# Two products with V side by side on TensorE, and one ScalarE copy for both

## The chip, the cores and the metric

The kernel runs on one core of one Trainium2 chip. The metric is the device time of one execution in microseconds (us), and the median of several executions is compared.

## The reference

The input is x of shape (16, 256, 256): 16 sequences of 256 tokens with 256 features. Three stages follow each other, each on a layer norm of x and added back to x.

```python
x = x + 0.5 * ffn(layernorm(x))     # 16 experts, each token goes to its best 2
x = x + attention(layernorm(x))     # 16 heads of 16, causal
x = x + 0.5 * ffn(layernorm(x))
```

The change touches attention only. For each batch (sequence) and head it computes `softmax(q k^T / 4 + causal mask) v`, the outputs of 16 heads are joined to 256 features and multiplied by `w_out`.

## The kernel before

Five engines run programs of their own and meet at semaphores: TensorE (PE) multiplies, VectorE (DVE) and ScalarE (ACT) read its outputs out of the eight banks of its output memory, GpSimd (POOL) masks and gathers rows, SyncE (SP) issues transfers. In attention the 16 batches are pipelined by hand. Each engine has a written-out order of steps (`PE_TURN`, `ACT_TURN`, `DVE_TURN`, `POOL_TURN`, `SP_TURN`), and `batches` runs through that list once per turn. An entry is (offset, kind, number): in turn i the step is done for batch i + offset, if there is such a batch. So one turn of PE holds steps of several batches. The waits are in the steps themselves (`after(engine, semaphore, count)`), and an engine that waits holds everything behind it in its list.

The steps of one batch that matter here:

- SCORE 0 to 11 (line 440, and one mask product at line 443). PE makes query by key scores in two banks in turn (bank 3 and 4), 4 heads at a time for n under 4 and 2 heads for the others. DVE takes the row maximum of each (line 590, also called SCORE). SCORE n on PE waits for the reduce of SCORE n-2 (`max_ready`), since it uses its bank.
- T 0 to 11 (line 465). PE makes the scores again, transposed (key by query), in banks 0, 1 and 2 in turn. ACT takes the exponential of each into `pr0` or `pr1` (line 537, also called T); both have two buffers. T n on PE waits for the exponential n-3. The exponentials of T 3g on ACT wait for the product PV g-2, which has read the same buffer.
- MASK on POOL (line 370) clears half a tile after the exponentials 1, 2, 4, 5, 7, 8, 10 and 11. Between these stand FETCH steps (line 346), which gather rows for a later batch.
- PV 0 to 3 (line 479). For a group of four heads PE multiplies the exponentials with V, each head in a strip of 32 columns of the array, into one half of `bankC`. PV n waits for 2n+2 masks. ACT copies that half to `oT` (line 525, also called PV), and the next PV waits for the copy.
- UN 0 and 1 (line 487) transpose `oT` back once all four copies are done (`oT_ready`). Then follow the division by the row sum on DVE (lines 608 and 610), TR and PR (lines 494 and 499), the product with `w_out`.
- V (line 427) makes V of a batch two later than the one whose PV stand in the same turn. ACT copies it (line 521) to `v_sb[b % 2]`, the buffer which the PV of that earlier batch read:

```python
elif kind == V:
    after(act, at["v_done"], b + 1)
    after(act, at["pv_done"], G * (b - 1))
```

- Q and K (line 420) multiply by the query and key weights, NORM (line 408) transposes the layer norm's output; ACT copies it (line 508). DVE splits q and k into bf16 parts: `LEFT_K` is line 580, `LOW_Q` and `LOW_K` line 585. In `DVE_TURN`, LEFT_K stands between the reduces of SCORE 3 and 4, LOW_Q between 5 and 6, and MIX (four instructions, lines 553 and 558, for a later batch) between 7 and 8.

Of the kernel before, what the change touches and what calls it, by code (L numbers as in the profile page):

```python
# [16 lines left out]
def macaron_block(nc, x_in, w_qkv, w_out, gate_w, gate_up, down, out, stages=("ffn", "attn", "ffn")):  # L17
    B, S, H = x_in.shape
# [30 lines left out]
    G = HEADS // 4  # L49
# [10 lines left out]
    with ctx:  # L60
# [124 lines left out]
        oT = sb("oT", [P, HEADS // 4, S])  # L185
# [89 lines left out]
        def exists(j):  # L275
# [9 lines left out]
        FETCH, MIX, MOMENTS, ROOT, NORM, Q, K, V = "fetch", "mix", "moments", "root", "norm", "q", "k", "v"  # L285
        HI_Q, HI_K, LEFT_Q, LEFT_K = "hi q", "hi k", "left q", "left k"
        MID_Q, MID_K, LOW_Q, LOW_K = "mid q", "mid k", "low q", "low k"
        SCORE, MAX, T, MASK, PV, UN, TR, PR = "score", "max", "scoreT", "mask", "pv", "untranspose", "transpose", "project"
        STATS = "stats"

        PE_TURN = [(-1, SCORE, 3), (-2, T, 5), (-2, T, 6), (-1, SCORE, 4), (-2, PV, 0), (-1, SCORE, 5), (-2, T, 7),
                   (-2, T, 8), (-1, SCORE, 6), (-2, T, 9), (-1, SCORE, 7), (-2, PV, 1), (-2, T, 10), (-2, T, 11),
                   (-1, SCORE, 8), (-1, SCORE, 9), (-2, PV, 2), (0, V, 0), (-2, PV, 3), (-1, SCORE, 10), (1, NORM, 0),
                   (-1, SCORE, 11), (-2, UN, 0), (-2, UN, 1), (1, Q, 0), (-1, MAX, 0), (-2, TR, 0), (1, K, 0),
                   (-2, TR, 1), (-2, PR, 0), (-2, PR, 1), (0, SCORE, 0), (-1, T, 0), (0, SCORE, 1), (-1, T, 1),
                   (-1, T, 2), (-1, T, 3), (0, SCORE, 2), (-1, T, 4)]
        ACT_TURN = [(12, MID_Q, 0), (12, HI_K, 0), (10, T, 0), (10, T, 1), (10, T, 2), (10, T, 3), (10, T, 4),
                    (10, T, 5), (10, T, 6), (10, PV, 0), (10, T, 7), (10, T, 8), (10, PV, 1), (10, T, 9), (10, T, 10),
                    (10, T, 11), (10, PV, 2), (12, MID_K, 0), (10, PV, 3), (12, V, 0), (13, NORM, 0), (11, MAX, 0),
                    (13, HI_Q, 0), (10, TR, 0), (10, TR, 1)]  # L300
        DVE_TURN = [(17, SCORE, 7), (20, MIX, 0), (17, SCORE, 8), (17, SCORE, 9), (18, LOW_K, 0), (20, MOMENTS, 0),
                    (17, SCORE, 10), (17, SCORE, 11), (16, UN, 0), (17, MAX, 0), (16, UN, 1), (20, NORM, 0),
# [17 lines left out]
        def after(eng, s, n):  # L320

            if n > 0:
                eng.wait_ge(s, n)
# [72 lines left out]
        def attn_tensor(pe):  # L396
# [5 lines left out]
            def part(kind, n, b):  # L402
# [8 lines left out]
                elif kind in (Q, K):  # L411
                    x, dst = OF[kind], (bankB, bankA)[OF[kind]]
                    after(pe, at["anT_ready"], b + 1)
                    if kind == Q:
                        after(pe, at["v_ready"], b)
                        if b == 0:
                            pe.wait_ge(ffn[0]["ye_ready"], NE_T)
                    for e in range(2):
                        for c in range(HC):
                            last = nc.tensor.matmul(dst[:, e * S:(e + 1) * S], wqk[:, c, x, e, :], anT[:, c, :],  # L420
                                                    start=(c == 0), stop=(c == HC - 1))
                    last.then_inc(at["qk_done"], 1)
                elif kind == V:
                    after(pe, at["left_ready"], 2 * b + 1)
                    for u in range(2):
                        for c in range(HC):
                            last = nc.tensor.matmul(bankB[:, u * H:(u + 1) * H], anT[:, c, u * P:(u + 1) * P], wv[:, c, :],  # L427
                                                    start=(c == 0), stop=(c == HC - 1))
                    last.then_inc(at["v_done"], 1)
                elif kind == SCORE:  # L430
                    u, h0, nh = score_of(n)
                    if n == 0:
                        after(pe, at["stacked_q"], 16 * SLOTS * (b + 1))
                        after(pe, at["stacked_k"], 16 * SLOTS * (b + 1))
                        after(pe, at["nmaxT_ready"], b)
                    after(pe, at["max_ready"], 3 * G * b + n - 1)
                    dst, w = bank[3 + n % 2], P * (u + 1)
                    q, k = qT[b % BUFS], kT[b % BUFS]
                    for i in range(nh):
                        nc.tensor.matmul(dst[:, i * w:(i + 1) * w], q[0:ROWS, h0 + i, u * P:(u + 1) * P], k[0:ROWS, h0 + i, 0:w],  # L440
                                         start=(i == 0), stop=False, skip_group_check=True)
                    diag = dst[:, :].rearrange("p (h k) -> p h k", k=w)[:, :, u * P:(u + 1) * P]
                    nc.tensor.matmul(diag, ident_b[:, :], future[:, 0:nh, :], start=False, stop=True,  # L443
                                     skip_group_check=True).then_inc(at["score_done"], 1)
                elif kind == MAX:
                    after(pe, at["nmax_ready"], b + 1)
                    for u in range(2):
                        last = nc.tensor.transpose(bank[3][:, :].bitcast(BF16)[0:3 * HEADS, u * P:(u + 1) * P], nmax[:, u, :],
                                                   ident_b[:, :])
                    last.then_inc(at["nmax_transposed"], 1)  # L450
                elif kind == T:
                    kt, h0, nh = scoreT_of(n)
                    if n == 0:
                        after(pe, at["maxed"], 16 * (b + 1))
                    if n < 2:
                        after(pe, at["x_done"], 2 * b + n - 1)
                    elif n == 2:
                        after(pe, at["attT_ready"], 2 * b)
                    else:
                        after(pe, at["exp_ready"], 3 * G * b + n - 2)  # L460
                    dst, w = bank[n % 3], S - kt * P
                    q, k = qT[b % BUFS], kT[b % BUFS]
                    for i in range(nh):
                        h = h0 + i
                        last = nc.tensor.matmul(dst[:, i * w:(i + 1) * w], k[0:ROWS + 3, h, kt * P:(kt + 1) * P],  # L465
                                                q[0:ROWS + 3, h, kt * P:S], start=(i == 0), stop=(i == nh - 1),
                                                skip_group_check=True)
                    last.then_inc(at["scoreT_done"], 1)
                elif kind == PV:
                    after(pe, at["masked"], 2 * G * b + 2 * n + 2)  # L470
                    after(pe, at["oT_ready"], G * b + n)
                    if n == 0:
                        after(pe, at["v_ready"], b + 1)
                        after(pe, at["attT_ready"], 2 * b - 1)
                    cols = n % 2 * S
                    for kt in range(2):
                        for j in range(4):
                            rhs = pr0[n % 2][:, j, :] if kt == 0 else pr1[n % 2][:, j, :]
                            last = nc.tensor.matmul(bankC[j * VW:(j + 1) * VW, cols + kt * P:cols + S],  # L479
                                                    v_sb[b % 2][:, kt, 4 * n + j, :], rhs, start=(kt == 0), stop=(kt == 1),  # L480
                                                    skip_group_check=True)
                    last.then_inc(at["pv_done"], 1)
                elif kind == UN:
                    after(pe, at["oT_ready"], G * (b + 1))
                    after(pe, at["exp_ready"], 3 * G * b + 10 + n)
                    for g in range(G):
                        last = nc.tensor.transpose(bank[n][:, g * P:(g + 1) * P], oT[:, g, n * P:(n + 1) * P], ident[:, :])  # L487
                    last.then_inc(at["o_transposed"], 1)
                elif kind == TR:
                    after(pe, at["att_ready"], 2 * b + n + 1)  # L490
                    if n:
                        after(pe, at["exp_ready"], 3 * G * (b + 1))
                    for c in range(HC):
                        last = nc.tensor.transpose((bankC, bank[2])[n][:, c * P:(c + 1) * P], att[:, n, c * P:(c + 1) * P], ident[:, :])
                    last.then_inc(at["att_transposed"], 1)
                elif kind == PR:
                    after(pe, at["attT_ready"], 2 * b + n + 1)
                    for c in range(HC):
                        last = nc.tensor.matmul(bank[n][:, 0:H], attT[:, n, c, :], wout_sb[:, c, :], start=(c == 0), stop=(c == HC - 1))  # L499
                    last.then_inc(at["proj_done"], 1)  # L500
            batches(PE_TURN, part)

        def attn_scalar(act):
            def part(kind, n, b):
# [17 lines left out]
                        .then_inc(at["v_ready"], 1)  # L522
                elif kind == PV:
                    after(act, at["pv_done"], G * b + n + 1)
                    nc.scalar.copy(oT[:, n, :], bankC[:, n % 2 * S:(n % 2 + 1) * S]).then_inc(at["oT_ready"], 1)
                elif kind == MAX:
                    after(act, at["nmax_transposed"], b + 1)
                    after(act, at["maxed"], 16 * b)
# [1 line left out]
                elif kind == T:  # L530
                    kt, h0, nh = scoreT_of(n)
                    g = n // 3
# [864 lines left out]
```

## Time and profile before

| | |
|---|---|
| median of 3 executions | 798.5 us (795.11, 798.5, 799.29) |
| the profiled execution | 797.04 us, span 795.3 us |
| PE busy over the span | 646.0 us (81%) |
| DVE, ACT, POOL busy | 517.8, 404.8, 398.1 us |
| granted clock of TensorE, mean | 0.914 |

The span reaches from the first to the last instruction; the execution's own time is 1.74 us longer. Busy times of engines overlap. The products PV stand in the trace from 246.3 to 546.5 us, and between them lie the 16 turns of attention that hold one batch's PV each.

### The profile page before, as it was taken

How to read it: one execution, taken by the hardware profiler on the slowest of the kernel's cores; microseconds unless marked ns; L12 is line 12 of the kernel's file. 1: busy time of each engine (PE TensorE's matmuls, PEld its weight loads, DVE VectorE, ACT ScalarE, POOL GpSimd, SP SyncE). 2: the span in 40 equal slices, each digit the busy share in tenths (PEclk: the TensorE clock that was granted, in tenths of full speed). 3: DMA queues.
4: the chain of work that ended last, by engine and by line, in shares of the span. 5: the costliest groups of instructions: out<-in, count | busy, mean ns of one | idle time of the engine just before them, and what ended most of it. 6: DMA issues, size and time to landing. Idle time of an engine off the chain costs nothing.

```text
span 795.3 us, 18007 instructions
## 1 busy us (share of the span) xinstructions
PE 646.0 (81%) x5502; PEld 526.3 (66%) x5503; DVE 517.8 (65%) x1407; ACT 404.8 (51%) x962; POOL 398.1 (50%) x466
## 2 busy tenths in 40 slices
PE   2728999998689999999999999987647999959300
PEld 2517999997456777777777777664436999959200
DVE  7887644444577888888888887763877444437442
ACT  1634577775216555555555555546612667736100
POOL 4123556664635555555555422224043777777474
PEclk9958999999889999999999999999857999979755
DMA  8792455657554444444444433300512566676654
GB/s 264 228 322 87 133 172 170 168 169 140 154 164 128 121 122 115 124 120 123 123 121 123 118 96 94 95 4 32 182 46 87 172 188 194 171 157 185 215 159 122
DMA packets 94160, 113.48 MB, mean 143 GB/s; under 512 B 11648, under 2 KB 84624, under 8 KB 94096
## 3 DMA queue, kind: packets, MB, share of 16 engines
q1 hardware_dynamic: 80240, 74.87, 29.7%
q0 software_dynamic: 13824, 37.77, 19.4%
q8 instruction: 37, 0.61, 0.3%
q14 instruction: 27, 0.22, 0.1%
q10 hardware_dynamic: 32, 0.02, 0.0%
HBM read 49.30 MB, written 33.55 MB: 104 GB/s over the span
## 4 chain that ended last, share of the span: by engine, by line
PE 68%; DVE 11%; POOL 6%; DMA 5%; issue 5%; ACT 3%; SPq 1%; DVEq 0%; POOLq 0%; ACTq 0%
PE bank L872 16%; PE bank L879 8%; PE bank L479 6%; PE bank L420 6%; PE bank L440 5%; PE bank L465 5%; PE bank L863 4%; PE bank L427 4%; POOL shared L711 4%; PE bank L499 3%; PE bank L443 3%; PE bank L487 2%; PE bank L841 1%; DMA spare<-normed,source 1%; DMA shared<-grouped_out,slot 1%
## 5 line engine op out<-in xcount | busy, mean ns | idle before, releaser
L700 POOL DMA_INDIRECT spare<-normed,source x128 | 123.5, 965 | 121.8 <-PE bank L863 56.5
L872 PE MATMUL bank<-xeT,shared 128*128 128x128 f32 x1280 | 175.6, 282 | 0.1
L872 PEld LDWEIGHTS bank<-xeT,shared 128*128 128x128 f32 x1280 | 162.0, 198 | 1.0 <-issue 0.9
L370 POOL TENSOR_SCALAR_AFFINE_SELECT pr<-pr 128x512 f32<-128x512 f32 x128 | 81.2, 658 | 155.1 <-ACT pr L537 155.1
L590 DVE TENSOR_REDUCE mx<-bank 128x2 f32<-128x512 f32 (+1 forms) x192 | 128.0, 687 | 25.9 <-PE bank L443 24.0
L1138 DVE TENSOR_TENSOR hid<-bank,silu 128x128 f32<-128x128 f32 x160 | 46.5, 291 | 121.5 <-ACT silu L992 121.2
L537 ACT ACTIVATE pr<-bank 128x512 f32<-128x512 f32 x192 | 102.8, 608 | 30.4 <-PE bank L465 18.0
L879 PE MATMUL bank<-wd_sb,hid 128*128 x320 | 99.5, 393 | 14.5 <-DVE hid L1138 14.4
L1002 ACT COPY shared<-wgu_sb 128x512 f32 x160 | 97.6, 611 | 26.4 <-DVE eid L1159 16.6
L992 ACT ACTIVATE silu<-bank 128x128 f32<-128x128 f32 x160 | 44.4, 278 | 75.5 <-PE bank L872 74.8
L988 ACT COPY xeT<-bank 128x256 f32<-128x256 f32 x160 | 59.9, 374 | 43.9 <-PE bank L863 36.0
L346 POOL DMA_INDIRECT gathered_rows<-grouped_out,slot x64 | 68.9, 1076 | 14.7 <-issue 9.5
L711 POOL DMA_INDIRECT shared<-grouped_out,slot x64 | 62.4, 975 | 27.4 <-issue 18.3
L1143 DVE COPY shared<-bank 128x256 f32<-128x256 f32 x160 | 66.9, 418 | 0.9 <-PE bank L879 0.5
L420 PE MATMUL bank<-anT,wqk 128*128 128x256 f32 x256 | 62.6, 390 | 1.7 <-ACT anT L508 1.7
L879 PEld LDWEIGHTS bank<-wd_sb,hid 128*128 128x128 f32 x320 | 49.9, 197 | 16.8 <-issue 16.5
L863 PE MATMUL bank<-ident,spare 128*128 128x128 f32 x256 | 50.8, 283 | 12.3 <-DMA spare<-normed,source 12.3
L443 PE MATMUL bank<-future,ident_b 128*128 128x256 bf16 (+1 forms) x192 | 59.4, 310 | 0.0
L479 PE MATMUL bank<-pr,v_sb 128*32 128x256 f32 (+1 forms) x1024 | 54.9, 332 | 3.4 <-POOL pr L370 3.4
L863 PEld LDWEIGHTS bank<-ident,spare 128*128 128x128 f32 x256 | 36.6, 147 | 26.1 <-issue 10.7
L440 PE MATMUL bank<-shared 112*128 112x256 bf16 (+1 forms) x352 | 50.5, 246 | 3.5 <-DVE mx L590 1.9
L420 PEld LDWEIGHTS bank<-anT,wqk 128*128 128x128 f32 x256 | 47.7, 196 | 8.3 <-ACT anT L508 2.6
(175 smaller groups left out, 1052.1 us busy)
## 6 DMA issues: line engine op xcount, KB each, us to landing
grouped_out<-shared SPq DMA_DIRECT2D x160, 128.0 KB
shared<-parts SPq DMA_DIRECT2D x154, 128.0 KB
spare<-parts SPq DMA_DIRECT2D x70, 128.0 KB
normed<-shared SPq DMA_DIRECT2D x16, 512.0 KB, 3.6
wgu_sb<-_L_ffn_gate_up_proj_dram SPq DMA_DIRECT2D x8, 512.0 KB, 8.9
out_dram<-x_sb SPq DMA_DIRECT2D x16, 256.0 KB, 2.9
x_sb<-in_L_attn_x_dram SPq DMA_DIRECT2D x3, 1024.0 KB, 10.1
wd_sb<-in_L_ffn_down_proj_dram SPq DMA_DIRECT2D x4, 512.0 KB, 9.2
```

Source lines behind the costliest of these rows:

```text
L420: last = nc.tensor.matmul(dst[:, e * S:(e + 1) * S], wqk[:, c, x, e, :], anT[:, c, :], start=(c == 0), stop=(c == HC - 1))
L440: nc.tensor.matmul(dst[:, i * w:(i + 1) * w], q[0:ROWS, h0 + i, u * P:(u + 1) * P], k[0:ROWS, h0 + i, 0:w], start=(i == 0), stop=False, sk ...
L443: nc.tensor.matmul(diag, ident_b[:, :], future[:, 0:nh, :], start=False, stop=True, skip_group_check=True).then_inc(at["score_done"], 1)
L479: last = nc.tensor.matmul(bankC[j * VW:(j + 1) * VW, cols + kt * P:cols + S], v_sb[b % 2][:, kt, 4 * n + j, :], rhs, start=(kt == 0), stop ...
L537: nc.scalar.activation(dst.rearrange("p h n -> p (h n)"), bank[n % 3][:, :], ACT.Exp).then_inc(at["exp_ready"], 1)
L590: nc.vector.tensor_reduce(mx[:, u, h0:h0 + nh], bank[3 + n % 2][:, :].rearrange("p (h k) -> p h k", h=nh), AX.X, ALU.max).then_inc(at["max ...
L700: nc.gpsimd.indirect_dma_start(xe[f][r], None, normed, bass.IndirectOffsetOnAxis(source[:, j:j + 1], 0)).then_inc(arrival(f, r), 16)
L711: nc.gpsimd.indirect_dma_start(late[:, t % LATE, j, :], None, grouped_out, bass.IndirectOffsetOnAxis(slot[:, t, j:j + 1], 0)).then_inc(at[ ...
L863: last = nc.tensor.transpose(bank[u][:, c * P:(c + 1) * P], xe[f][r][:, c * P:(c + 1) * P], ident[:, :])
L872: last = nc.tensor.matmul(bank[2 + u][:, h * P:(h + 1) * P], wgu_tile[u][:, c, h * I:(h + 1) * I], xeT[:, u, c, :], start=(c == 0), stop=( ...
L879: nc.tensor.matmul(bank[6 + u][:, 0:H], hid[:, u, :], wd_sb[:, e, :], start=True, stop=True).then_inc(s["down_done"], 1)
L1002: nc.scalar.copy(wgu_tile[u][:, :, :], wgu_sb[:, e, :, :]).then_inc(s["weights_ready"], 1)
```

## The change

The lists of PE and ACT are reordered, and two copies become one. `DVE_TURN`, `POOL_TURN` and `SP_TURN` stay.

On PE, T and SCORE alternate from SCORE 3 on; PV 0 and PV 1 stand together behind T 8, and PV 2 and PV 3 together behind SCORE 10, where V stood between them before. ACT has one step behind each pair: it copies the whole of `bankC` (512 columns) to two groups of `oT`, and `oT_ready` counts pairs. On ACT the first of these now stands behind the exponential 8, and the second behind the copy of V, where the copies before stood ahead of it.

```diff
-        PE_TURN = [(-1, SCORE, 3), (-2, T, 5), (-2, T, 6), (-1, SCORE, 4), (-2, PV, 0), (-1, SCORE, 5), (-2, T, 7),
-                   (-2, T, 8), (-1, SCORE, 6), (-2, T, 9), (-1, SCORE, 7), (-2, PV, 1), (-2, T, 10), (-2, T, 11),
-                   (-1, SCORE, 8), (-1, SCORE, 9), (-2, PV, 2), (0, V, 0), (-2, PV, 3), (-1, SCORE, 10), (1, NORM, 0),
+        PE_TURN = [(-1, SCORE, 3), (-2, T, 5), (-1, SCORE, 4), (-2, T, 6), (-1, SCORE, 5), (-2, T, 7), (-1, SCORE, 6), (-2, T, 8),
+                   (-2, PV, 0), (-2, PV, 1), (-1, SCORE, 7), (-2, T, 9), (-2, T, 10), (-1, SCORE, 8), (-2, T, 11), (-1, SCORE, 9),
+                   (0, V, 0), (-1, SCORE, 10), (-2, PV, 2), (-2, PV, 3), (1, NORM, 0),
                    (-1, SCORE, 11), (-2, UN, 0), (-2, UN, 1), (1, Q, 0), (-1, MAX, 0), (-2, TR, 0), (1, K, 0),
...
-                    (10, T, 5), (10, T, 6), (10, PV, 0), (10, T, 7), (10, T, 8), (10, PV, 1), (10, T, 9), (10, T, 10),
-                    (10, T, 11), (10, PV, 2), (12, MID_K, 0), (10, PV, 3), (12, V, 0), (13, NORM, 0), (11, MAX, 0),
+                    (10, T, 5), (10, T, 6), (10, T, 7), (10, T, 8), (10, PV, 1), (10, T, 9), (10, T, 10),
+                    (10, T, 11), (12, MID_K, 0), (12, V, 0), (10, PV, 3), (13, NORM, 0), (11, MAX, 0),
...
-                    after(pe, at["oT_ready"], G * b + n)
+                    after(pe, at["oT_ready"], (G * b + n) // 2)
...
-                    after(pe, at["oT_ready"], G * (b + 1))
+                    after(pe, at["oT_ready"], G // 2 * (b + 1))
...
-                    nc.scalar.copy(oT[:, n, :], bankC[:, n % 2 * S:(n % 2 + 1) * S]).then_inc(at["oT_ready"], 1)
+                    nc.scalar.copy(oT[:, n - 1:n + 1, :].rearrange("p g n -> p (g n)"), bankC[:, :]).then_inc(at["oT_ready"], 1)
```

## Rows read from the trace of the kernel before

**Rows 1.** Stretches: busy PE, PEld, DVE, ACT, POOL (counts); granted clock; DMA share; GB/s.

```profile
335.00:354.85 19.85, 19.85 (x192) 15.08 (x191) 17.70 (x47) 11.68 (x26) 10.35 (x13) 1.00 0.41 118
...
580.70:604.00 23.30, 12.64 (x69) 9.61 (x66) 18.09 (x63) 4.98 (x12) 13.77 (x15) 0.57 0.26 77
```

**Rows 2.** Timeline of PE in that turn: start, length, line; x is the count.

```profile
345.51 0.38 PE L443 MATMUL bank<-future,ident_b 128*128 128x512 bf16 x1
345.73 0.67 PE L465 MATMUL bank<-spare 115*128 115x128 bf16 x6
...
346.46 0.27 PE L443 MATMUL bank<-future,ident_b 128*128 128x256 bf16 x1
346.66 0.86 PE L479 MATMUL bank<-pr,v_sb 128*32 128x256 f32 x16
347.45 0.39 PE L440 MATMUL bank<-shared 112*128 112x256 bf16 x2
...
347.80 0.60 PE L465 MATMUL bank<-spare 115*128 115x256 bf16 x6
...
352.00 1.99 PE L427 MATMUL bank<-wv,anT 128*128 128x256 f32 x8
353.92 0.86 PE L479 MATMUL bank<-pr,v_sb 128*32 128x256 f32 x16
```

**Rows 3.** Timeline inside PV 0: its last four matmuls, of 128 columns each.

```profile
347.23 0.29 PE L479 MATMUL bank<-pr,v_sb 128*32 128x128 f32 x4
```

**Rows 4.** The chain that ended last, turn before: starts and lengths of PE's pieces.

```profile
315.54 0.44 PE bank L408 x4
...
319.50 1.73 PE bank L420 x8
...
328.56 0.22 PE bank L440 x2
328.78 0.11 PE bank L443
328.89 0.22 PE bank L465 x2
```

**Rows 5.** Timeline of DVE in that turn; in brackets the wait and what ended it.

```profile
345.27 1.36 DVE L590 TENSOR_REDUCE mx<-bank 128x4 f32<-128x512 f32 x2 [0.41 <-PE bank L443]
346.54 0.68 DVE L580 TENSOR_TENSOR left<-bank,parts 128x512 f32<-128x512 f32 x1
347.13 0.68 DVE L590 TENSOR_REDUCE mx<-bank 128x2 f32<-128x512 f32 x1
...
350.40 0.87 DVE L553 SCALAR_TENSOR_TENSOR mix<-gathered_rows,weight,x_sb 128x256 f32<-128x256 f32 x2
...
351.98 1.28 DVE L590 TENSOR_REDUCE mx<-bank 128x2 f32<-128x512 f32 x2
```

**Rows 6.** Timeline of ACT in that turn and ahead of it.

```profile
335.28 0.59 ACT L521 COPY v_sb<-bank 128x512 f32<-128x512 f32 x1
...
347.65 0.60 ACT L537 ACTIVATE pr<-bank 128x512 f32<-128x512 f32 x1 [0.71 <-PE bank L479]
348.14 0.37 ACT L525 COPY oT<-bank 128x256 f32<-128x256 f32 x1
348.39 1.10 ACT L537 ACTIVATE pr<-bank 128x512 f32<-128x512 f32 x2
```

**Rows 7.** Timeline of POOL in that turn.

```profile
349.18 1.23 POOL L370 TENSOR_SCALAR_AFFINE_SELECT pr<-pr 128x512 f32<-128x512 f32 x2 [0.25 <-ACT pr L537]
350.55 1.15 POOL L346 DMA_INDIRECT gathered_rows<-grouped_out,slot  x1
351.70 1.44 POOL L370 TENSOR_SCALAR_AFFINE_SELECT pr<-pr 128x512 f32<-128x512 f32 x2
```

**Rows 8.** Timeline of the last turn: ACT's last copy to `oT` and PE behind it.

```profile
546.88 0.37 ACT L525 COPY oT<-bank 128x256 f32<-128x256 f32 x1 [1.55 <-PE bank L479]
...
547.30 1.09 PE L487 MATMUL bank<-ident,oT 128*128 128x128 f32 x8 [0.49 <-ACT oT L525]
```

## The prediction, made before the changed kernel ran

> **What bounds the kernel now.** I read the stretches first: in one turn of attention, 19.85 us long, PE is busy for all of it at a granted clock of 1.00, DVE for 17.70, ACT for 11.68 and POOL for 10.35 [rows 1]. The reader is to see that PE leaves nothing free, that DVE is second with some 2 us of slack in a turn, and that ACT, where two copies become one, has eight. The chain that ended last agrees: in such a turn every piece of it is PE's [rows 4]. Then the timeline of PE, for the places where it starts late, and those of DVE, ACT and POOL, for how soon each could release it in the new order. So a saving counts only where it shortens PE's queue, and each new wait of PE counts in full, in every turn. All times below are of the turn at 335 to 355 us.
>
> **What the change takes away from PE.** PV is the step in strips of 32 columns, and around it PE has gaps. The mask product ahead of PV 0 starts at 346.46 and such a piece takes 0.11 [rows 2, 4], so PV could start at 346.57; it starts at 346.66: 0.09 lost. Its last four matmuls, of 128 columns in four strips at once, start at 347.23 [rows 3]; a pair of matmuls of 256 columns takes 0.22 [rows 4], so 256 columns 0.11, and each product here is in two matmuls of f32 one after the other. I take 0.11 for the last 128 columns, so the array is fed until 347.34. The next step starts at 347.45 [rows 2]: 0.11 lost. Thus PV is 0.68 of feeding and 0.20 of gaps. Before, there are four such PV; after, two pairs, in which the second PV follows the first after 0.68. That saves 2 x 0.20 = 0.40 a turn. V behind PV takes from 352.00 to 353.92, 1.92 [rows 2], where the same eight matmuls in Q take 1.73 [rows 4]; 0.09 of the 0.19 is PV's entry, counted above, and 0.10 is lost with V's first weights. V no longer follows a PV: 0.10. SCORE behind PV takes 0.35 (347.45 to 347.80) in place of 0.33; one such place fewer: 0.02. T 6 also waits now: T 5, T 6 and the first half of SCORE 4 need 3 x 0.22 = 0.66 and take from 345.73 to 346.46, 0.73; T 6 is later in the new order, so 0.07 goes. Together 0.59 a turn.
>
> **What the merged copy is worth.** ACT goes from one copy to an exponential in 0.25 us (348.14 to 348.39) [rows 6], so two copies hold it for about 0.5. For 512 columns the interval is about that of an exponential: two last 1.10 and one 0.60 to 0.61, so 0.49. I cost the merge at nothing, since ACT idles 8 us a turn; the copy's result, though, comes 0.59 after its start (the copy of V, 512 columns) and not 0.37. The Trainium skill, in "TensorEngine Tiling (Array Packing)", section PSUM Bottleneck, advises to read PSUM across several tiles of a bank at once, because evacuation may be the limit after packing. If ACT were the limit, 0.37 + 0.37 - 0.59 = 0.15 a pair would come off the path, 0.3 a turn, and the loss below would be 0.57 a turn and not 0.87. The rows show that ACT is not the limit, and the sum has nothing for it.
>
> **The first new wait: SCORE 6.** Nothing in the beginning of the turn moves up to SCORE 3 and T 5. DVE's reduces of SCORE 2 and 3 end at 345.27 + 1.36 = 346.63, LEFT_K follows at 346.54 (an instruction starts shortly before the end of the one before), the reduce of SCORE 4 at 347.13, ending at 347.81 [rows 5]. This chain can't start sooner, as it waited for PE at its head, and its order is not changed. PE starts 0.05 after a release (547.25 to 547.30) [rows 8]. So SCORE 6 can't start before 347.86. Before, PV 0 stood in this interval and filled it. Now PE has T 5, SCORE 4, T 6, SCORE 5, T 7 from 345.73 on: 3 x 0.22 + 2 x 0.33 = 1.32 [rows 4], until 347.05. Some of the difference is waited at SCORE 4 and 5 for the reduces of 2 and 3, the rest at SCORE 6; together 0.81 a turn. PV 0 can't fill it since it stands behind T 8, and T 8 behind SCORE 6.
>
> **The second: T 10.** Take PV 0's start as zero. PE: PV 1 at 0.68, SCORE 7 at 0.68 + 0.79 = 1.47, T 9 at 1.82, T 10 ready at 2.04. ACT: the exponential 6 uses the buffer that PV 0 reads, PV 0 ends at 0.86 [rows 2] and ACT starts 0.13 after (347.52 to 347.65) [rows 2, 6]: 0.99. Exponential 7 starts at 1.48 and ends at 2.09, T 10 starts at 2.14: a wait of 0.10. T 9 (exponential 6 ends at 1.59) and T 11 (exponential 8 at 2.58, PE there at 2.69) don't wait.
>
> **DVE and POOL behind it.** SCORE 7 ends at about 1.98, its reduce starts at 2.02, MIX 0.60 later takes 1.58 (350.40 to 351.98), the reduce of SCORE 8 starts at 4.20 and ends at 4.88 [rows 5]. PE comes to SCORE 10 at 2.69 + 0.22 (T 11) + 0.33 (SCORE 9) + 1.73 (V) = 4.97, and could start at 4.93: no wait, by 0.04. Then PV 2 at 4.97 + 0.33 + 0.09 = 5.39 and PV 3 at 6.07. PV 3 needs mask 11. Mask 7 starts 0.17 after exponential 7, at 2.26; the gather 1.37 later (349.18 to 350.55), mask 10 1.15 after that, at 4.78; both masks are through 1.23 to 1.44 later, 6.01 to 6.22 [rows 7]. So PV 3 waits between 0 and 0.20. The longer pair runs beside MIX in the rows, and in the new order MIX is past by then; I take 0. The gather stands only in the first 11 of 16 turns.
>
> **The third: UN 0.** ACT's copy of V waits for all PV of the batch two before, PV 3 among them, whose buffer it writes. Before, the copy for PV 3 stood ahead of it; now it stands behind it. Counted from PV 3's start: PV 3 ends at 0.86, the copy of V starts at 0.99, the copy to `oT` 0.48 later at 1.47 and ends at 2.06 [rows 6], UN 0 may start at 2.11. PE is through PV 3 and its gap (0.79), NORM (0.44) and SCORE 11 (0.33) [rows 4] at 1.56. The wait is 0.55. Behind UN the turn goes on as before: the copy for NORM and Q have room of some 0.4 us.
>
> **Sum.** Waits 0.81 + 0.10 + 0.55 = 1.46, savings 0.59: 0.87 us longer a turn. Fourteen of the sixteen turns with PV have all this: 12.2 us. The last two lack V and LEFT_K; for them I take 0.65 each, between 0 and 0.87. In all 13.5 us. The profiled execution would go from 797.04 to 810.5 us, its span from 795.3 to 808.8. It is 1.5 us below the median shown, so the median would be 798.5 + 13.5 = 812.0 us. The stages before and after attention are not touched.
>
> **Rivals.**
> (1) SCORE 6 is not held. If DVE's chain came 0.81 us sooner, or PE 0.81 later, this wait is nothing and a turn costs 0.87 - 0.81 = 0.06: with 0.6 for the ends 799.9 us, no slower that can be measured. For it: DVE has 2 us of slack over a turn. Against it: the chain begins with an idle DVE that PE releases, so the slack is not there. It decides from a wait under 0.3. Chance 0.08.
> (2) The tail is hidden: UN 0 isn't late, since the copy of V gets through early. A turn costs 0.32: 798.5 + 4.5 + 0.9 = 803.9. Against it stands the count in the code. Chance 0.10.
> (3) The change does what its words say and no wait shows: 16 x 0.59 = 9.4 us less, 789.1. For it: ACT and POOL are half idle. It needs both waits gone. Chance 0.05.
> (4) POOL or DVE are later than taken: PV 3 waits 0.20 for its mask in 11 turns and SCORE 10 as much for MIX, so 2.2 to 4.4 more: 814 to 816.5. Chance 0.11.
> (5) The clock. Granted is 1.00 with PE full, and 0.57 where PE is busy for 12.64 of 23.30 us [rows 1]. PE would now be idle 1.46 of 20.7 us, far less. Were a twentieth of the 330 us at 1.2 GHz, it would cost some 8 us: 820. Chance 0.04. The Trainium skill, "TensorE: Matmul & The Clock Gate", section "HAM oscillation", says that waits between bursts of matmuls can put the engine back to the slow clock each time; no row here shows it for waits this short.
>
> **How the numbers follow.** The forecast has 0.62, and by itself reaches from 809 to 815 (a tenth of a us either way in the gaps and releases, twice a turn). Those who measure this kernel can tell about 0.5%, 4 us, from no change. Slower by more: 0.62 + 0.10 + 0.11 + 0.04 = 0.87; within: 0.08; faster: 0.05. The range from 800 to 819 leaves out rival 3, rival 5 and half of rival 1, and some misjudgment in the forecast.
>
> **What would show it.** In a turn of the new trace: a turn of 20.7 us and not 19.84; PE idle ahead of line 440, released by DVE's line 590, for 0.6 us or more; line 479 with 32 matmuls in 1.4 to 1.55 us, twice a turn; PE idle 0.5 us ahead of line 487, released by ACT's line 525; the copy at line 521 ahead of 525. ACT's copies of 0.59 us, 32 of them. The forecast is wrong if PE is busy all through, if the second PV of a pair also has a gap of 0.2, or if the turn's length is under 20.2.

## The result: slower by 3%, and the profile after

The changed kernel takes 821.41 us (median of 4 executions, 819.82 to 826.33) where the kernel before takes 798.89 (median of 4). The ratio is 1.0296, 95% interval 1.0261 to 1.0332: slower, by 22.5 us between the medians. The forecast was 13.5 us slower, 812.0, with a range to 819. The sign was right, and so were the three waits that were forecast; a fourth, which the sum had at nothing, is 0.8 us a turn.

The page of the changed kernel: busy time, share of the span, instructions.

```profile
span 824.6 us, 17974 instructions
...
PE 653.2 (79%) x5502; PEld 528.1 (64%) x5503; DVE 527.3 (64%) x1407; ACT 397.3 (48%) x930; POOL 398.4 (48%) x466
```

Busy PE hardly grew (646.0 to 653.2) and ACT fell by 7.5 us, while the span grew by 29.3. The instructions are the same but for 32 copies: the time went into waiting. Of the 29.3 us, 23.3 lie between the first and the last turn's division by the row sum (315.0 in place of 291.7), 3.0 ahead of it and 3.0 behind. The profiled execution is the longest of the four, and TensorE's granted clock accounts for part of it: from 540.07 us on it was at half, 1.2 GHz, for 3.4 us, and again for 6.8 us from 570.8 on, where the kernel before had 1.00 all through attention. In the two microseconds ahead of the first fall PE was busy for 0.39 and 0.48 us. This is the stretch, with the columns of [rows 1]:

```profile
540.00:545.00 5.00, 5.00 (x25) 3.68 (x24) 2.10 (x6) 1.24 (x4) 0.00 (x0) 0.66 0.03 8
```

One turn, with the same columns, and then who waited for whom in it (us in total, times, longest):

```profile
338.36:359.92 21.56, 20.13 (x192) 15.05 (x191) 18.53 (x47) 11.24 (x25) 10.30 (x14) 1.00 0.39 112
```

```profile
PEld bank L440 <- DVE mx L590: 2.0, 3, 1.0
PE bank L440 <- DVE mx L590: 1.1, 2, 0.6
...
PEld bank L487 <- ACT oT L525: 0.6, 1, 0.6
...
PE bank L487 <- ACT oT L525: 0.3, 1, 0.3
```

A turn takes 21.56 us, not 19.84 [rows 1] and not the 20.71 forecast. PE waits for DVE at SCORE and for ACT at UN. The timeline of PE, for [rows 2], shows where:

```profile
354.68 0.39 PE L465 MATMUL bank<-spare 115*128 115x128 bf16 x4
...
355.97 0.38 PE L465 MATMUL bank<-spare 115*128 115x256 bf16 x2
356.83 0.39 PE L440 MATMUL bank<-shared 112*128 112x256 bf16 x2 [0.47 <-DVE mx L590]
357.06 0.27 PE L443 MATMUL bank<-future,ident_b 128*128 128x256 bf16 x1
357.17 0.39 PE L465 MATMUL bank<-spare 115*128 115x128 bf16 x4
357.49 1.51 PE L479 MATMUL bank<-pr,v_sb 128*32 128x256 f32 x32
358.93 0.39 PE L440 MATMUL bank<-shared 112*128 112x256 bf16 x2
...
359.27 0.73 PE L465 MATMUL bank<-spare 115*128 115x256 bf16 x4
359.84 0.39 PE L440 MATMUL bank<-shared 112*128 112x256 bf16 x2
...
360.73 1.89 PE L427 MATMUL bank<-wv,anT 128*128 128x256 f32 x8
363.25 0.39 PE L440 MATMUL bank<-shared 112*128 112x256 bf16 x2 [0.63 <-DVE mx L590]
363.48 0.27 PE L443 MATMUL bank<-future,ident_b 128*128 128x256 bf16 x1
363.68 1.51 PE L479 MATMUL bank<-pr,v_sb 128*32 128x256 f32 x32
365.12 0.65 PE L408 MATMUL bank<-ident,an 128*128 128x128 f32 x4
...
366.44 1.09 PE L487 MATMUL bank<-ident,oT 128*128 128x128 f32 x8 [0.33 <-ACT oT L525]
```

The pair of PV takes 1.44 us from its start to the next step's (357.49 to 358.93), where two separate ones took 2 x 0.79 and a gap of 0.09 each [rows 2]: the saving is real. Around it stand four waits. SCORE 6 starts at 356.83, 0.86 after T 7 where 0.22 is T 7's. SCORE 8 starts at 359.84, 0.57 after T 9, where T 9 and T 10 are 0.44: 0.13 of waiting at T 10. SCORE 10 starts at 363.25, 2.52 after V where V is 1.73. UN 0 starts at 366.44, 1.32 after NORM where NORM and SCORE 11 are 0.77. The timeline of DVE, for [rows 5]:

```profile
354.22 1.36 DVE L590 TENSOR_REDUCE mx<-bank 128x4 f32<-128x512 f32 x2 [0.41 <-PE bank L443]
355.49 0.68 DVE L580 TENSOR_TENSOR left<-bank,parts 128x512 f32<-128x512 f32 x1
356.09 1.28 DVE L590 TENSOR_REDUCE mx<-bank 128x2 f32<-128x512 f32 x2
...
359.47 0.69 DVE L590 TENSOR_REDUCE mx<-bank 128x2 f32<-128x512 f32 x1 [0.90 <-PE bank L443]
360.08 1.33 DVE L553 SCALAR_TENSOR_TENSOR mix<-gathered_rows,weight,x_sb 128x256 f32<-128x256 f32 x2
361.32 1.27 DVE L558 SCALAR_TENSOR_TENSOR x_sb<-gathered_rows,weight,mix 128x256 f32<-128x256 f32 x2
362.52 1.27 DVE L590 TENSOR_REDUCE mx<-bank 128x2 f32<-128x512 f32 x2
```

MIX lasts from 360.08 to 362.59, 2.5 us, and the reduce of SCORE 8 starts 2.44 after MIX does; in [rows 5] it was 1.58. Taken one by one, two of its four instructions are much longer, and the two masks beside them too. (The first, beside the end of mask 7, takes 0.56.) The second of each line of MIX, and POOL's masks 8 and 10:

```profile
360.56 0.85 DVE L553 SCALAR_TENSOR_TENSOR mix<-gathered_rows,weight,x_sb 128x256 f32<-128x256 f32 x1
...
361.72 0.87 DVE L558 SCALAR_TENSOR_TENSOR x_sb<-gathered_rows,weight,mix 128x256 f32<-128x256 f32 x1
```

```profile
360.31 0.82 POOL L370 TENSOR_SCALAR_AFFINE_SELECT pr<-pr 128x512 f32<-128x512 f32 x1
...
362.23 0.85 POOL L370 TENSOR_SCALAR_AFFINE_SELECT pr<-pr 128x512 f32<-128x512 f32 x1
```

An instruction of MIX that stands alone takes 0.48, a mask 0.64. Each of the four overlaps an instruction of the other engine and takes 0.2 to 0.4 us more. In [rows 7] one pair of masks, 1.44, was already long beside MIX; the prediction read that as a price of POOL's only, and in that turn MIX did keep its 1.66. ACT at the end of the turn, for [rows 6]:

```profile
365.31 0.58 ACT L521 COPY v_sb<-bank 128x512 f32<-128x512 f32 x1 [2.81 <-PE bank L479]
365.80 0.59 ACT L525 COPY oT<-bank 128x512 f32<-128x512 f32 x1
```

V's product had long been there; its copy waits for PV 3 (2.81 us), and the copy that UN 0 needs stands behind it.

### The profile page after: what moved, and what is told of

Its sections match the earlier page's. It is cut to its first block, busy times and chain, and to the rows that moved or that the text cites. A ratio compares the mean times of both kernels' runs of the same rounds, so it can differ in the third digit from the quotient of the medians.

```text
span 824.6 us, 17974 instructions
## 1 busy us (share of the span) xinstructions
PE 653.2 (79%) x5502; PEld 528.1 (64%) x5503; DVE 527.3 (64%) x1407; ACT 397.3 (48%) x930; POOL 398.4 (48%) x466
## 4 chain that ended last, share of the span: by engine, by line
PE 54%; DVE 21%; POOL 10%; issue 6%; DMA 4%; ACT 4%; SPq 0%; DVEq 0%; POOLq 0%; ACTq 0%
PE bank L872 14%; POOL shared L711 7%; PE bank L879 6%; PE bank L420 6%; DVE mx L590 6%; PE bank L479 5%; PE bank L440 4%; PE bank L863 4%; PE bank L499 3%; PE bank L465 2%; PE bank L443 2%; PE bank L487 2%; DVE mix L553 2%; DVE x_sb L558 2%; PE bank L841 1%
## 5 line engine op out<-in xcount | busy, mean ns | idle before, releaser
L346 POOL DMA_INDIRECT gathered_rows<-grouped_out,slot x64 | 67.0, 1047 | 14.9 <-issue 14.6
L440 PE MATMUL bank<-shared 112*128 112x256 bf16 (+1 forms) x352 | 52.5, 252 | 15.8 <-DVE mx L590 11.1
L420 PE MATMUL bank<-anT,wqk 128*128 128x256 f32 x256 | 60.6, 381 | 1.7 <-ACT anT L508 1.7
L479 PE MATMUL bank<-pr,v_sb 128*32 128x256 f32 (+1 forms) x1024 | 49.5, 332 | 2.1 <-POOL pr L370 2.1
```

## The experiments

The first four and the last three ran on chips where the kernel before took 801 to 802 us (medians of 13 and 22 executions). The middle six ran on two chips where it took 863.46 and 862.4: in the traces from there the stage behind attention is some 60 us longer, attention isn't. So ratios are compared, each to the kernel before on the same chip, and the length of a turn in each trace. A turn is counted from the first reciprocal of one batch's UN to the next batch's. The table has the turns with MIX and gathers; where the first half of the turn is that of before, the third of them is longer by 0.8 to 1.3 us and left out (20.97 in the kernel before).

| kernel | turn, us | MIX, us | ratio to before | 95% interval |
|---|---|---|---|---|
| before | 19.84 | 1.66 | 1 | |
| changed | 21.56 | 2.52 | 1.0296 | 1.0261 to 1.0332 |
| copies merged alone | 19.84 | 1.66 | 0.9991 | 0.9965 to 1.0018 |
| PV 3's copy ahead of V's | 21.17 | 2.52 | 1.0243 | 1.0193 to 1.0293 |
| MIX ahead of SCORE 7's reduce | 21.39 | 1.66 | 1.0299 | 1.0255 to 1.0342 |
| masks of 8 columns | 20.76 | 1.66 | 1.0149 | 1.0104 to 1.0193 |
| first half alone | 20.86 to 21.12 | 2.52 | 1.0171 | 1.0118 to 1.0223 |
| second half alone | 20.10 to 20.38 | 1.66 | 1.0054 | 1.0022 to 1.0086 |
| first pair ahead of SCORE 6 | 21.25 | 3.05 | 1.0192 | 1.0160 to 1.0224 |
| the same, V early | 20.66 | 3.05 | 1.0102 | 1.0068 to 1.0137 |
| the same, MIX and STATS exchanged | 19.65 to 21.43 | 1.66 | 1.0099 | 1.0067 to 1.0131 |
| before, MIX and STATS exchanged | 19.59 to 20.16, mostly 19.84 | 1.66 | 1.0009 | 0.9988 to 1.0030 |
| LEFT_K later | 20.98 | 2.52 | 1.0194 | 1.0154 to 1.0234 |
| three causes taken away | 19.80, every fourth 21.3 | 1.66 | 1.0048 | 1.0022 to 1.0074 |
| second pair alone, mended | 19.51 | 1.66 | 0.9931 | 0.9910 to 0.9951 |

**The copies merged, and nothing else.** PE's list is that of before.

```diff
-                    (10, T, 5), (10, T, 6), (10, PV, 0), (10, T, 7), (10, T, 8), (10, PV, 1), (10, T, 9), (10, T, 10),
-                    (10, T, 11), (10, PV, 2), (12, MID_K, 0), (10, PV, 3), (12, V, 0), (13, NORM, 0), (11, MAX, 0),
+                    (10, T, 5), (10, T, 6), (10, T, 7), (10, T, 8), (10, PV, 1), (10, T, 9), (10, T, 10),
+                    (10, T, 11), (12, MID_K, 0), (10, PV, 3), (12, V, 0), (13, NORM, 0), (11, MAX, 0),
```

> The kernel before with only the copies merged: PE's order is that of before, ACT copies the whole bank behind PV 1 and behind PV 3. My theory, that ACT's copies have slack and that the loss comes from PE's new order: the pair's copy for PV 1 ends at 350.07 + 0.07 + 0.59 = 350.73 and PV 2 starts at 351.21, so nothing is held there; behind PV 3 the longer copy ends 0.22 later, and UN 0 has some 0.3 us of room. No change in a turn (19.84 us), 797 to 801 us. Rival, that the merged copy itself costs (its result comes later): 0.2 us or more a turn, 802 us or more.

19.84 us a turn and no measurable change. With PE's order of before the merged copy neither costs nor gives anything measurable; the loss is in the orders.

**PV 3's copy ahead of V's**, in the changed kernel's `ACT_TURN`.

```diff
-(12, V, 0), (10, PV, 3)
+(10, PV, 3), (12, V, 0)
```

> The changed kernel with one swap in ACT's list: the copy for PV 3 stands ahead of the copy of V. Theory: UN 0 waits for that copy behind the copy of V, 0.5 us a turn; with the swap the copy ends 0.86 + 0.07 + 0.59 us after PV 3's start and UN 0 needn't wait. A turn goes from 21.56 to 21.1 us, the time down by 6 to 7.5 us against the changed kernel, to about 814. Rival, that this wait only hides another one behind it (the maximum's transposes, the copy for NORM): under 2 us.

A turn falls by 0.39 us to 21.17, near the 21.1 expected. The ratio falls from 1.0296 to 1.0243, which is 4 us and not 6 to 7.5, and the intervals overlap, so the gain is shown by the turns and not by the times. No PE wait at line 487 is left in its turn. The wait was there; 0.1 us of the 0.5 came back at Q, which takes 1.93 us from UN's end in place of 1.82.

**MIX one place up**, in the changed kernel's `DVE_TURN`.

```diff
-DVE_TURN = [(17, SCORE, 7), (20, MIX, 0),
+DVE_TURN = [(20, MIX, 0), (17, SCORE, 7),
```

> The changed kernel with MIX moved one place up in DVE's list, ahead of the reduce of SCORE 7, where DVE idles 0.9 us in a turn and POOL isn't masking. Theory: MIX takes 2.5 us in the changed kernel because it runs beside POOL's masks 7 and 8, and 1.6 us away from them. It then starts at the end of the reduce of SCORE 6 and takes 1.6; the reduce of SCORE 7 starts 0.6 us later than now, SCORE 9 waits 0.4 us for it, SCORE 10 doesn't wait. A turn goes from 21.56 to about 21.15, 4 to 5 us less than the changed kernel. Rival, MIX is slow for what it reads and not for its neighbours: it still takes 2.5 us, SCORE 9 waits 1.3 us, and the time goes up by 5 us.

MIX is back at 1.66 us in every turn, so it isn't slow for what it reads. But a turn falls by only 0.17 us where 0.4 was expected, and the time not at all. SCORE 9 waits 0.41 us, as expected, and counted from PV 0, SCORE 10 comes 0.37 us earlier. Then 0.13 us is given back at the second pair (1.57 us from its start to NORM's, with mask 11 late) and the rest at the tail. The neighbours of the masks have changed: LOW_K on DVE, two inputs in SBUF, now runs beside masks 10 and 11. These are DVE and POOL of that kernel:

```profile
365.06 1.00 DVE L585 TENSOR_TENSOR parts<-left,parts 128x512 bf16<-128x512 f32 x1 [0.50 <-ACT parts L517]
```

```profile
364.87 1.69 POOL L370 TENSOR_SCALAR_AFFINE_SELECT pr<-pr 128x512 f32<-128x512 f32 x2
```

LOW_K takes 1.00 in place of 0.68, the pair of masks 1.69 in place of 1.23.

**Masks of 8 columns.** The changed kernel with the causal mask over 8 of 128 columns only.

```diff
-                    m = (pr1 if second else pr0)[g % 2][:, :, 0:P]
+                    m = (pr1 if second else pr0)[g % 2][:, :, 0:8]
...
-                                            pattern=[[0, 4], [1, P]], channel_multiplier=-1).then_inc(at["masked"], 1)
+                                            pattern=[[0, 4], [1, 8]], channel_multiplier=-1).then_inc(at["masked"], 1)
```

> The changed kernel with POOL's masks over 8 of 128 columns (the rest of the causal mask is left out). Each mask is an instruction of some 0.1 to 0.2 us in place of 0.64. Theory, MIX is slowed by POOL's masks beside it: MIX takes 1.6 us again, SCORE 10 waits less than 0.1 us, a turn goes from 21.56 to about 20.75 us, and the time falls by some 9 to 10 us to 812. Rival, it is the gather (its descriptors) or ACT that slow MIX: MIX stays at 2.4 us, and the time falls by less than 2 us.

MIX and the turn are as the theory said. The narrow masks take 0.43 us each and not 0.1 to 0.2, and the ratio falls by 1.5%, somewhat more than 9 to 10 us. The instructions of MIX's second line over the whole program (count, shortest, median, longest in ns) in the changed kernel, and with narrow masks:

```profile
L558 DVE SCALAR_TENSOR_TENSOR x_sb<-gathered_rows,weight,mix x32: 471/476/873, 197.4 to 491.1; 128x256 f32<-128x256 f32 x32
```

```profile
L558 DVE SCALAR_TENSOR_TENSOR x_sb<-gathered_rows,weight,mix x32: 471/478/489, 198.4 to 483.3; 128x256 f32<-128x256 f32 x32
```

The longest goes from 873 to 489 ns, a turn from 21.56 to 20.76. That is the 20.71 of the forecast, which had MIX at its old length. The gather, which is still there, isn't the neighbour that matters.

**Each half of the change alone.** The first has the new order up to SCORE 9 with one copy for PV 0 and PV 1, and then the old; the second has the old order up to SCORE 9 and then the new.

```diff
 first half alone, against the changed kernel
-                   (0, V, 0), (-1, SCORE, 10), (-2, PV, 2), (-2, PV, 3), (1, NORM, 0),
+                   (-2, PV, 2), (0, V, 0), (-2, PV, 3), (-1, SCORE, 10), (1, NORM, 0),
 second half alone, against the kernel before
-                   (-1, SCORE, 8), (-1, SCORE, 9), (-2, PV, 2), (0, V, 0), (-2, PV, 3), (-1, SCORE, 10), (1, NORM, 0),
+                   (-1, SCORE, 8), (-1, SCORE, 9), (0, V, 0), (-1, SCORE, 10), (-2, PV, 2), (-2, PV, 3), (1, NORM, 0),
```

> Only the first half of the change: SCORE and T alternate, PV 0 and PV 1 together with one copy; PV 2, V, PV 3 and SCORE 10 stand as in the kernel before, with single copies. Theory (waits add up along PE's list): SCORE 4 to 6 wait 0.81 us for DVE's reduces, T 10 0.10, PV 2 some 0.2 to 0.5 for its mask; the pair saves 0.20 and T 6 0.07; SCORE 10 stands behind V and two PV and has no wait for the reduce that MIX delays. A turn of 20.7 to 21.0 us, 812 to 817 us. Rival, the MIX collision costs wherever it stands: 21.4 us or more a turn, 822 us.

> Only the second half of the change: V and SCORE 10 go ahead of the pair PV 2, PV 3 with one copy behind V's copy; the first half stands as in the kernel before. Theory: UN 0 waits 0.5 us for the copy behind V's, the pair saves 0.20 and V 0.10; DVE isn't behind, MIX keeps its place away from the masks, SCORE 10 doesn't wait. A turn of 20.05 to 20.1 us, 3 to 4.5 us slower than before, 802 to 805. Rival, that SCORE 10 ahead of the pair waits for the reduce of SCORE 8 here too: 20.8 us a turn, 813.

The first half adds some 1.15 us a turn, the second 0.3 to 0.5; together the change adds 1.72. MIX is long with the first half and not with the second: it is the first half that moves it beside the masks. With that half alone, SCORE 10 stands late enough in PE's list not to wait; there PV 2 waits 0.36 us for mask 8, one of the masks that MIX slows. The second half puts SCORE 10 ahead of the pair. So the 0.79 us at SCORE 10 need both halves, while each alone has waits that the other hides, and the sums don't simply add. The second half adds 0.2 us more than expected; in its turns ACT saw PV 3's end 0.3 to 0.4 us after its row ended (last section).

**The first pair in the gap.** PE's list has both PV ahead of SCORE 6, and ACT copies PV 3 before V; the second kernel also has V ahead of SCORE 9 and SCORE 10 behind the second pair.

```diff
+(-1, SCORE, 3), (-2, T, 5), (-2, T, 6), (-1, SCORE, 4), (-2, T, 7), (-1, SCORE, 5), (-2, T, 8),
+(-2, PV, 0), (-2, PV, 1), (-1, SCORE, 6), (-2, T, 9), (-1, SCORE, 7), (-2, T, 10), (-2, T, 11), (-1, SCORE, 8),
+(-1, SCORE, 9), (0, V, 0), (-1, SCORE, 10), (-2, PV, 2), (-2, PV, 3), (1, NORM, 0),
 and with V early, the last line
+(0, V, 0), (-1, SCORE, 9), (-2, PV, 2), (-2, PV, 3), (-1, SCORE, 10), (1, NORM, 0),
```

> The changed kernel with the pair PV 0, PV 1 ahead of SCORE 6 (order SCORE 3, T 5, T 6, SCORE 4, T 7, SCORE 5, T 8, PV 0, PV 1, SCORE 6, T 9, SCORE 7, T 10, T 11, SCORE 8, SCORE 9), and the copy for PV 3 ahead of V's. Theory: the pair fills the time in which DVE does LEFT_K and the reduce of SCORE 4, so SCORE 6 has no wait; left are 0.1 to 0.2 us at SCORE 9 and at SCORE 10, and the pairs' saving of 0.5 to 0.6. A turn of 19.5 to 19.8 us if MIX stays clear of the masks, 1 to 5 us faster than before. Rival, MIX collides with the masks, SCORE 10 waits 0.8 us: 20.3 us a turn, 6 us slower than before.

> As the kernel with the pair ahead of SCORE 6, and V goes ahead of SCORE 9, SCORE 10 behind the pair PV 2, PV 3. Theory: SCORE 9 no longer waits for the reduce of SCORE 7, nor SCORE 10 for that of SCORE 8, even if MIX takes 2.5 us. A turn of 19.3 to 19.5 us, 5 to 9 us faster than before, 790 to 794 us. Rival, that something else ends last (mask 11 for PV 3, or the maximum of SCORE 11 behind a later DVE): no faster than the kernel before.

Both rivals won, the first by more than it said: 21.25 us a turn and 1.9% slower, not 20.3 and 6 us. MIX lies so that it meets three masks and takes 3.05 us; SCORE 10 is 1.48 us late for its reduce, or, with SCORE 10 out of the way, the maximum behind SCORE 11 waits instead (PE idles 0.6 us at line 448). In the turns in which no MIX is left the second kernel takes 18.98 and 19.17 us, under the 19.84 and 19.66 of before.

**MIX and STATS exchanged**, in that last kernel, and in the kernel before as a control.

```diff
-DVE_TURN = [(17, SCORE, 7), (20, MIX, 0), (17, SCORE, 8), (17, SCORE, 9), (18, LOW_K, 0), (20, MOMENTS, 0),
+DVE_TURN = [(17, SCORE, 7), (15, STATS, 0), (17, SCORE, 8), (17, SCORE, 9), (18, LOW_K, 0), (20, MOMENTS, 0),
...
-                    (19, LEFT_Q, 0), (15, STATS, 0),
+                    (19, LEFT_Q, 0), (21, MIX, 0),
```

> The kernel with the pair ahead of SCORE 6, V ahead of SCORE 9 and SCORE 10 behind the second pair (20.66 us a turn), and in DVE's list MIX and STATS change places: MIX now stands behind LEFT_Q, one turn ahead of MOMENTS, where POOL masks nothing; STATS stands behind the reduce of SCORE 7. Theory: all of MIX's 3.05 us in that kernel beyond 1.66 was waiting for POOL's masks and POOL's for it; MIX takes 1.66 us, DVE is no longer late for the maximum behind SCORE 11, and a turn takes 18.9 to 19.3 us (its turns without MIX took 18.98 and 19.17). Against the kernel before, 19.84 us a turn: 7 to 12 us faster. Rival: DVE has too much to do in 19 us (17.7 us busy), and whatever is moved comes back as a wait: no faster than before.

> The kernel before with the same swap of MIX and STATS in DVE's list, and nothing else. Theory: PE is full in every turn of the kernel before, so the swap gives nothing there: 19.84 us a turn, within 0.3% of the kernel before (the one turn of 20.97 us may go). Rival, the swap itself is what makes the other kernel faster: 7 us or more here too.

MIX takes 1.66 us in all turns, as the theory had it, and the kernel isn't faster than before, as the rival had it: plain turns take 20.25 and every fourth, in which STATS carries seven small instructions more, 21.4. Some of it is the late end of PV 3 as ACT sees it: UN 0 comes 0.49 us late in a plain turn. The control is as fast as the kernel before, and its third turn is still long (20.66, and 20.16 behind it), though MIX takes 1.66 there.

**LEFT_K later; all three causes taken away.** LEFT_K goes behind the reduce of SCORE 5. The second kernel adds the exchange of MIX and STATS and PV 3's copy ahead of V's.

```diff
-(18, SCORE, 3), (19, LEFT_K, 0), (18, SCORE, 4), (18, SCORE, 5)
+(18, SCORE, 3), (18, SCORE, 4), (18, SCORE, 5), (19, LEFT_K, 0)
```

> The changed kernel with LEFT_K two places later in DVE's list, behind the reduce of SCORE 5. Theory: of the 0.8 us that PE waits at SCORE 4 to 6, 0.6 are LEFT_K's place between the reduces of SCORE 3 and 4; SCORE 6 then waits 0.05 us. A turn goes from 21.56 to 20.9 to 21.0 us, 8 to 9 us less than the changed kernel (1.0% of 800). Rival: the wait only moves on to SCORE 8 or T 10, since DVE has the same to do: 21.3 us or more.

> The changed kernel with all three causes taken away: LEFT_K behind the reduce of SCORE 5, MIX and STATS exchanged so that MIX runs where POOL doesn't mask, and the copy for PV 3 ahead of V's. Theory, the three add up: 21.56 - 0.6 - 0.8 - 0.4 = 19.75 us a turn, within 0.4% of the kernel before. If the three are all there is, what is left above 19.25 (19.84 less the saving of 0.59) is T 10's wait and a tenth or two at the scores. Rival: they hide one another and a turn stays above 20.3 us, 1% slower than before.

PE with LEFT_K later, T 7 and SCORE 6: 0.28 us apart, where it was 0.86.

```profile
352.32 0.38 PE L465 MATMUL bank<-spare 115*128 115x256 bf16 x2
352.60 0.39 PE L440 MATMUL bank<-shared 112*128 112x256 bf16 x2
```

A turn is 20.98, the 0.6 us expected. With all three, plain turns take 19.80 (19.75 expected), and the 1.5 us more in every fourth turn make the kernel 0.5% slower than before: with STATS in its new place, DVE's seven further instructions there hold one SCORE on PE for 1.3 us. In the plain turns SCORE 10 and UN 0 don't wait at all.

**The second pair alone, with its waits mended.** The first half is that of before.

```diff
-(-1, SCORE, 8), (-1, SCORE, 9), (-2, PV, 2), (0, V, 0), (-2, PV, 3), (-1, SCORE, 10), (1, NORM, 0),
+(-1, SCORE, 8), (-1, SCORE, 9), (0, V, 0), (-2, PV, 2), (-2, PV, 3), (-1, SCORE, 10), (1, NORM, 0),
...
-(10, PV, 2), (12, MID_K, 0), (10, PV, 3), (12, V, 0)
+(12, MID_K, 0), (10, PV, 3), (12, V, 0)
```

> The kernel before with PV 2 and PV 3 as a pair and one copy for both; V stands ahead of the pair, SCORE 10 between the pair and NORM, and ACT copies the pair ahead of V. The first half of the turn is that of before. Theory: the pair saves 0.20 and V 0.10 us, and UN 0 has NORM, SCORE 11 and SCORE 10 (1.1 us) to cover the copy, so no wait: 19.5 us a turn, 4 to 5 us (0.5 to 0.6%) faster than before. Rival: the pair's end reaches ACT late (as in the kernel with only the second half changed, where the copy began 0.36 us after the last product and not 0.12), and the gain is under 2 us.

PE and ACT of that kernel:

```profile
352.61 1.51 PE L479 MATMUL bank<-pr,v_sb 128*32 128x256 f32 x32
354.05 0.39 PE L440 MATMUL bank<-shared 112*128 112x256 bf16 x2
354.28 0.28 PE L443 MATMUL bank<-future,ident_b 128*128 128x256 bf16 x1
354.39 0.60 PE L408 MATMUL bank<-ident,an 128*128 128x128 f32 x4
...
355.16 1.04 PE L487 MATMUL bank<-ident,oT 128*128 128x128 f32 x8
```

```profile
354.25 0.59 ACT L526 COPY oT<-bank 128x512 f32<-128x512 f32 x1 [2.10 <-PE bank L479]
```

The copy ends at 354.84 and UN 0 starts at 355.16 without a wait. 19.51 us a turn where 19.5 was expected, and 0.7% faster than the kernel before: the only version that is faster than before and not only than the changed one.

## Why the prediction was wrong in size

The sum went wrong at one term above all: it took MIX's length from another place in the turn and so had no wait at SCORE 10. The terms in their order:

**PE's savings: right.** 0.59 us a turn were forecast, 0.30 of them for the second pair with V. The kernel with that pair alone gained 0.33 a turn. The forecast had 1.56 us for a pair with its gaps, of which 1.47 lie behind its start; measured are 1.44. One PV takes 0.79 to the next step and a pair 1.44, so the second adds 0.65 and not 0.68, and 0.14, not 0.11, is lost behind a PV. The forecast overlooked 0.06 at NORM, which now stands behind a PV (0.49 in place of 0.43), and as much inside UN.

**The merged copy at nothing: right**, as far as the kernel that has only that can show it (0.9991, 0.9965 to 1.0018).

**SCORE 6, 0.81 us: right.** In the trace, T 5 to SCORE 6 take 2.15 us (354.68, where T 5 starts, to 356.83) for 1.32 of work: 0.83. That LEFT_K is in that chain is shown: two places later, 0.58 us of a turn go.

**T 10, 0.10 us: right in the trace, 0.13** (0.57 less 0.44). No run changed it by itself.

**UN 0, 0.55 us: right in place, 0.55 in the trace** (1.32 less 0.77, of which NORM is 0.06), and 0.39 of a turn came off when the copies changed places.

**SCORE 10, no wait "by 0.04": this step failed.** It took MIX's 1.58 us from a turn in which MIX started after mask 8, and moved it to where masks 8 and 10 run. MIX took 2.44 to the next reduce, 0.86 more, and SCORE 10 waited 0.79 us for the reduce of SCORE 8. With that the turn adds up: 20.71 + 0.86 - 0.04 = 21.53, measured 21.56. Rival 4 named this wait but priced it at 0.20. The prediction also had MIX past when mask 10 runs; it wasn't (MIX ends at 362.59, mask 10 starts at 362.23). PV 3 had no wait for its mask, as forecast, but PE had by then lost its 0.79 us at SCORE 10, so that was partly luck.

The kernel before had shown MIX's price in one of its sixteen turns, which the prediction left unread. There, MIX met masks 7 and 8 and took 2.56 us in place of 1.66:

```profile
309.59 1.40 DVE L553 SCALAR_TENSOR_TENSOR mix<-gathered_rows,weight,x_sb 128x256 f32<-128x256 f32 x2
310.91 1.24 DVE L558 SCALAR_TENSOR_TENSOR x_sb<-gathered_rows,weight,mix 128x256 f32<-128x256 f32 x2
```

```profile
309.95 1.53 POOL L370 TENSOR_SCALAR_AFFINE_SELECT pr<-pr 128x512 f32<-128x512 f32 x2
```

That turn took 20.97 us, but not mainly for MIX. PE waited in it once, for a mask:

```profile
PE bank L479 <- POOL pr L370: 1.1, 1, 1.1
```

The gather ahead of masks 7 and 8 started 1.94 us after the mask in front of it, where it is 0.14 in the next turn, and the two masks took 0.3 us more beside MIX. In the control kernel, where MIX is elsewhere, the gather is as late and most of the excess stays. Why it is late isn't shown.

That the masks are what makes MIX long is shown by the narrow ones; that MIX's inputs play a part is only suggested, by LOW_K, which also reads two tensors in SBUF, and by the reduce of SCORE 7, which reads a bank and overlaps mask 7: it takes 0.69 us and the mask 0.63, like alone. The Trainium skill says it, in "GPSIMD Engine Reference", section Specifications: POOL shares its SBUF interfaces with VectorE, and they contend when a VectorE instruction has two inputs in SBUF. The traces agree: 0.48 to 0.85 us for such an instruction beside a mask.

**The sum.** The forecast had 12.6 us between the first and the last division, and it is 23.3. The eleven turns with MIX and gathers took 17.7 more than before and not 9.6; this is the wait at SCORE 10. (Each took 1.72 more than 19.84, but the kernel before had its one long turn among them.) The two turns after, in which MIX is gone, took 2.0 more, where 1.7 was forecast. The last two added 3.6 us in the profiled execution and not 1.3, and the clock row above covers part: in the kernel with PV 3's copy first, at full clock there, they added 1.1. The term "0.65 each" for these two had no rows behind it. The remaining 6.0 us of the profiled execution lie outside. Ahead of the first PV, PE waited 4.6 us for one transfer, where it was 1.3 before; the second stretch at half clock reaches 3.2 us behind the last division. Whether the new order has a part in either isn't shown. The medians lie 22.5 us apart, not 29.3. Rival 5's clock did turn up, but in the last turns and for 3.4 us, not in a twentieth of attention.

## What to carry to other kernels

Before an instruction is moved in time, look up what the engine that shares its memory does at the new place, not only what its own engine does; its duration belongs to the neighbourhood it was measured in. An instruction that is longer in one turn of the old trace than in the others is worth reading: it may price what the change will do in every turn. And a saving on a full engine is kept only if the work it displaced from a gap (here PV from the time DVE needs for LEFT_K) isn't what hid someone else's latency.

## What the runs showed of the hardware

Here DVE's instructions with two SBUF inputs and POOL's masks slowed each other: MIX's from 0.48 to 0.85 us, LOW_K from 0.68 to 1.00, and a mask from 0.64 to 0.82 or 0.85. Four instructions of MIX took 1.66 us alone, 2.52 beside the end of one mask and two more, and 3.05 in the kernels where they lay beside three. A gather on POOL beside them, without masks of full width, left them at 1.66.

A PV, in strips of 32 columns, left 0.09 us open ahead of it between full-width products. It took 0.79 us to the next step where a second PV behind it added only 0.65, so 0.14 more was lost behind it. V lost 0.10 more behind one and NORM 0.06.

In some orders ACT got PV's end late. In the kernel with the pair in the gap and MIX and STATS exchanged, PE's row ends at 406.41, and ACT's copy, which waits for it alone, starts 0.88 us later, not 0.07 as behind every PV 3 of the kernel with PV 3's copy first:

```profile
404.90 1.51 PE L479 MATMUL bank<-pr,v_sb 128*32 128x256 f32 x32
```

```profile
407.29 0.59 ACT L525 COPY oT<-bank 128x512 f32<-128x512 f32 x1 [2.70 <-PE bank L479]
```

The ends of matmuls are modelled in this profile, so the product itself may have run late. The trace's semaphore events speak for that: SCORE 10, whose row ends at 406.84, was released at 407.32, just behind PV 3 at 407.26. It was so in most turns with gathers of the first-half kernel and of the two with V early (0.5 to 0.9 us) and of the second-half kernel (mostly 0.3 to 0.4), and not in the changed kernel nor in the first one with the pair in the gap. What causes it stays open.
